# Reciprocals of softmax sums spread over partitions by DMA in a two-layer transformer kernel

## What is computed

```python
def _L0_attn_ref(x, norm_scale, wq, wk, wv, w_out, b_out):
    h = _rmsnorm(x, norm_scale)
    q = jnp.einsum('bsd,dhe->bshe', h, wq)
    k = jnp.einsum('bsd,dhe->bshe', h, wk)
    v = jnp.einsum('bsd,dhe->bshe', h, wv)
    q = (q * scale).astype(softmax_dtype)
    weights = jnp.einsum('bqhd,bkhd->bhqk', q, kf)
    weights = jax.nn.softmax(weights, axis=-1).astype(dtype)
    new_vals = jnp.einsum('bhqk,bkhd->bqhd', weights, v).astype(dtype)
    out = jnp.einsum('bqhe,hed->bqd', new_vals, w_out) + b_out
    return out
```

## Time and profile before

| | |
|---|---|
| median of 3 runs | 1432.15 us (1431.54 to 1432.47) |
| the profiled execution's own time | 1431.51 us |
| its span, first to last instruction | 1429.7 us |
| instructions | 33458 |
| period of the main loop | 84.85 us |
| TensorE's granted clock, mean | 0.988 of full speed |

### The profile page before, as it was taken

The page is one execution under the profiler, slowest core; times in us unless marked ns, Lnnn a source line. Parts: engine busy times, 40 slices in busy tenths (PEclk is TensorE's granted clock), DMA queues, the critical chain, the costliest instruction groups (busy, mean ns, idle before and its releaser), DMA issues.

```text
span 1429.7 us, 33458 instructions
## 1 busy us (share of the span) xinstructions
PE 1366.9 (96%) x11456; PEld 1202.2 (84%) x11456; DVE 925.6 (65%) x2535; ACT 904.3 (63%) x2492; POOL 502.5 (35%) x409
## 2 busy tenths in 40 slices
PE   6897999999999999999999999999999999999867
PEld 4685989888898988889898898988889898888767
DVE  4366576675766757566675757667576675756684
ACT  6675766757577575766657576675757657575423
POOL 3307062350705316071440706235070531607100
PEclk9999999999999999999999999999999999999988
DMA  7000000000000000000000000000000000000000
GB/s 262 5 1 5 1 2 8 0 7 0 0 7 0 7 0 0 7 0 7 0 7 0 0 7 0 7 0 7 0 0 7 0 7 0 0 5 1 5 1 8
DMA packets 13944, 13.77 MB, mean 10 GB/s; under 512 B 1609, under 2 KB 12754, under 8 KB 13650
## 3 DMA queue, kind: packets, MB, share of 16 engines
q1 hardware_dynamic: 13906, 13.27, 2.9%
HBM read 11.17 MB, written 2.10 MB: 9 GB/s over the span
## 4 chain that ended last, share of the span: by engine, by line
PE 64%; issue 11%; DVE 8%; ACT 4%; DVEq 4%; POOL 3%; POOLq 2%; SPq 1%; DMA 1%; ACTq 0%
PE bank_F L1208 14%; PE bank_S L1081 6%; DVEq L346 4%; PE bank_T L1067 4%; PE bank_T L1122 4%; PE bank_A L1135 4%; PE bank_T L1068 3%; PE bank_T L1069 3%; PE bank_F L1067 3%; ACT probs L573 3%; PE bank_F L1068 3%; PE bank_F L1069 3%; PE bank_A L1146 3%; PE bank_A L1067 3%; PE bank_A L1068 3%
## 5 line engine op out<-in xcount | busy, mean ns | idle before, releaser
L1208 PE MATMUL bank_F<-down,hid 128*128 128x128 f32 x2944 | 357.5, 277 | 5.4 <-DVE x L790 4.6
L1208 PEld LDWEIGHTS bank_F<-down,hid 128*128 128x128 f32 x2944 | 342.0, 192 | 14.7 <-DVE x L790 8.3
L573 ACT ACTIVATE probs<-bank_S,neg_max 128x256 f32<-128x256 f32 x512 | 236.2, 476 | 140.7 <-DVE neg_max L711 140.7
L711 DVE TENSOR_REDUCE neg_max<-bank_S 128x2 f32<-128x512 f32 x256 | 164.6, 684 | 96.1 <-PE bank_S L1081 96.0
L790 DVE SCALAR_TENSOR_TENSOR x<-bank_F,gates,x 128x128 f32<-128x128 f32 x496 | 149.8, 343 | 42.5 <-PE bank_F L1208 32.6
L491 POOL TENSOR_TENSOR hid<-hid,qkv 128x1024 f32<-128x1024 f32 x60 | 169.2, 2831 | 22.6 <-ACT hid L589 22.6
L461 POOL TENSOR_TENSOR mean_sq<-sum_sq,one_over_d 128x2 f32<-128x2 f32 x16 | 3.1, 197 | 442.8 <-ACT h_row L547 442.8
L552 ACT ACTIVATE probsT<-bank_T 128x512 f32<-128x512 f32 x256 | 139.6, 606 | 27.8 <-PE bank_T L1122 27.8
L479 POOL TENSOR_TENSOR hid<-qkv 128x1024 f32<-128x1024 f32 x45 | 121.1, 2690 | 69.3 <-ACT qkv L552 69.3
L1146 PE MATMUL bank_A<-probsT,values 128*64 128x256 f32 x1024 | 139.6, 394 | 1.1 <-ACT probsT L552 1.0
L1122 PE MATMUL bank_T<-ident,probs 128*128 128x128 f32 x1024 | 138.3, 278 | 0.2 <-ACT probs L573 0.2
(11 more groups left out here) (187 smaller groups left out, 3133.2 us busy)
## 6 DMA issues: line engine op xcount, KB each, us to landing
x_row<-in_x SPq DMA_DIRECT2D x16, 128.0 KB, 2.2
hid<-in_w SPq DMA_DIRECT2D x1, 2048.0 KB, 9.1
down<-in_w SPq DMA_DIRECT2D x1, 2048.0 KB, 14.3
out<-x SPq DMA_DIRECT2D x16, 128.0 KB, 1.8
hid<-in_rw SPq DMA_DIRECT2D x1, 1024.0 KB, 7.3
hid<-in_wv SPq DMA_DIRECT2D x1, 512.0 KB, 3.9
hid<-in_wq SPq DMA_DIRECT2D x1, 512.0 KB, 5.1
hid<-in_wk SPq DMA_DIRECT2D x1, 512.0 KB, 5.8
```

Source lines behind the costliest of these rows:

```text
L573: ins = sc.activation(probs[:, h // 2 % 2, h % 2, t, :], unit.bank(f"S{h}")[:, t * S:(t + 1) * S], ACT.Exp, bias=neg_max[:, h, t:t + 1], a ...
L711: ve.tensor_reduce(neg_max[:, h, :], v.bank(f"S{h}")[:, :].rearrange("p (t k) -> p t k", t=NT), AX.X, ALU.max, negate=True).then_inc(max_r ...
L1208: ins = te.matmul(bank[:, (j * NT + t) * P:(j * NT + t + 1) * P], hid[:, e, k, tokens(t)], down[:, e, k, :], start=k == 0, stop=k == m - 1)
```

## The change

The reciprocals no longer go through ScalarE and TensorE. SP stores `sum_inv` of a pair (128 partitions x 4 values) to a small DRAM buffer, `sums_apart`, so that the 256 tokens of each head lie one behind the other there. Once this store has landed, SP loads each head's 256 values to 64 partitions (a source step of 0), two loads per pair, into `inv_spread`. VectorE's `o_scale` then multiplies the bank of `O` directly with `inv_spread` and writes `oT`. Both buffers have two slots, by the parity of s. `o_out`, `repeat_inverse` and `spread` are gone with their semaphores, and VectorE's reciprocal waits until the store of two pairs ago has landed. SP's body is written out for all 18 iterations in place of the hardware loop. The two loads of 2 MB move from SP's `load_late` to ScalarE, behind the first pair's copies in iteration 0.

```diff
-        row_inv = sb("row_inv", P, 2, NT, 2, DH)
+        sums_apart = nc.dram_tensor("sums_apart", [2, 2, S], F32).ap()
+        inv_spread = sb("inv_spread", P, 2, S)
...
-                load(4, up1_loaded, w1_in)
-                load(4, down1[:], w2_in)
+
+            def spread_inverse(v, s):
+
+                sp.wait_ge(inverse_ready, v.at(0, HP, s + 1))
+                if v.it > 0 or s >= 2:
+                    sp.wait_ge(inverse_spread, v.at(0, 32 * HP, 32 * max(s - 1, 0)))
+                sp.dma_start(sums_apart[s % 2].rearrange("j (t p) -> p (j t)", t=NT), sum_inv[:, s % 2, :], allow_slow_non_contiguous=True).then_inc(inverse_stored, 16)
+                sp.wait_ge(inverse_stored, v.at(0, 16 * HP, 16 * (s + 1)))
+                if s >= 2:
+                    sp.wait_ge(*v.drain(f"O{s - 2}"))
+                elif v.it > 0:
+                    sp.wait_ge(*v.previous().drain(f"O{HP - 2 + s}"))
+                for j in range(2):
+                    src = sums_apart[s % 2, j]
+                    sp.dma_start(inv_spread[j * DH:(j + 1) * DH, s % 2, :], bass.AP(src.tensor, src.offset, [[0, DH], [1, S]])).then_inc(inverse_spread, 16)
...
+                if v.a:
+                    for s in range(HP):
+                        spread_inverse(v, s)
                 if v.c:
                     sp.wait_ge(ln_ready[3], v.at(2, 1, 1))
...
-            run(sp, body)
+            for it in range(ROWS + 2):
+                body(Iteration(it, 0, banks))
...
-            def o_out(v, s):
-
-                act.wait_ge(*v.fill(f"O{s}"))
-                sc.activation(oT(s), v.bank(f"O{s}")[:, 0:S], ACT.Copy).then_inc(o_copied, 1)
...
-            def repeat_inverse(v, s):
-
-                act.wait_ge(inverse_ready, v.at(0, HP, s + 1))
-                sc.activation(row_inv[:, s % 2], sum_inv[:, s % 2].rearrange("p (j t a) -> p t j a", j=2, a=1).broadcast_to([P, NT, 2, DH]),
-                              ACT.Copy).then_inc(repeated_ready, 1)
...
                     if v.a and s == HP - 2:
-                        o_out(v, s - 1)
-                        repeat_inverse(v, s)
                         transposed_probs(v, s)
...
+                    if v.it == 0 and s == 0:
+                        for dst, src in loads1:
+                            act.dma_start(dst, src).then_inc(loaded[4], 16)
...
+                if v.it > 0 or s >= 2:
+                    dve.wait_ge(inverse_stored, v.at(0, 16 * HP, 16 * max(s - 1, 0)))
                 settled(dve, ve.reciprocal(sum_inv[:, s % 2, :], row_sum[:, s % 2, :]).then_inc(inverse_ready, 1))
...
-                dve.wait_ge(o_copied, v.at(0, HP, s + 1))
-                ve.tensor_tensor(oT(s), oT(s), v.bank(f"O{s}")[:, S:2 * S], ALU.mult).then_inc(v.drain(f"O{s}")[0], 1)
+                dve.wait_ge(*v.fill(f"O{s}"))
+                dve.wait_ge(inverse_spread, v.at(0, 32 * HP, 32 * (s + 1)))
+                ve.tensor_tensor(oT(s), v.bank(f"O{s}")[:, 0:S], inv_spread[:, s % 2, :], ALU.mult).then_inc(v.drain(f"O{s}")[0], 1)
...
-            def spread(v, s):
-
-                bank = v.bank(f"O{s}")
-                pe.wait_ge(*v.drain(f"O{s}", before=1))
-                pe.wait_ge(repeated_ready, v.at(0, HP, s + 1))
-                for t in range(NT):
-                    te.transpose(bank[:, S + t * P:S + (t + 1) * P], row_inv[:, s % 2, t].rearrange("p j e -> p (j e)"), ident[:])
...
-                    if name[0] == "S" and bank == "S0" and v.nth.get(f"O{int(name[1:]) // 2 - 2}"):
-                        spread(v, int(name[1:]) // 2 - 2)
```

More of the change, by code:

```diff
@@ L314, in transformer_blocks @@
         inverse_ready = sem("inverse_ready")
-        repeated_ready = sem("repeated_ready")
-        o_copied = sem("o_copied")
+        inverse_stored = sem("inverse_stored")
+        inverse_spread = sem("inverse_spread")
         max_ready = sem("max_ready")
@@ L362, in weights_and_values @@
                     qkv1[:, t, :, 2, :].rearrange("p g (a d) -> p a d g", a=1).broadcast_to(full))
-        n_loads = [0] * 5
+        loads1 = (up1_loaded, w1_in), (down1[:], w2_in)
+        n_loads = [0, 0, 0, 0, 16 * len(loads1)]
         def wait_weights(eng, v, group):
@@ L654, in body @@
                         softmax_exp(v, 2 * s + 3)
-                    if v.a and s >= 1 and s != HP - 2:
-                        o_out(v, s - 1)
-                    if v.a and s != HP - 2:
-                        repeat_inverse(v, s)
                     if v.b and s == 1:
@@ L673, in body @@
                     head_exp(v, 1)
-                if v.a:
-                    o_out(v, HP - 1)
                 sc.activation(table_load[:], table_load[:], ACT.Gelu)
@@ L1138, in unit @@
                     s = int(name[1:])
-                    if s >= HP - 2:
-                        spread(v, s)
                     for j in range(2):
```

## The result

The changed kernel takes 2094.6 us (median of 4 runs, 2086.16 to 2100.63), against 1432.31 us before (1431.54 to 1433.03): 1.462 times as long, 95% interval 1.4567 to 1.4672. The forecast was 1394, with a range to 1418. It is 662 us slower, where 38 us faster was forecast.

What follows compares the result with a forecast made beforehand. TensorE was taken to bound the loops. Removed transposes 32 us, the output projection's wait 3 and the first row 3 made 38 us off 1431.5, forecast 1394 us as the runs' median, range 1379 to 1418.

Steps and rivals of the forecast that it cites:

- What the removed transposes cost: Main loop, TensorE: removing two `spread` transposes per head pair saves 1.98 us per row, 32 us over 16 rows.
- The alternative of 40 us: TensorE, same transposes: if the 0.09 us behind each `spread` went as well, removal would save 40 us.
- What bounds the kernel: Main loop: TensorE is busy 84.41 of 84.85 us per period, so work taken off it comes off the time.
- GpSimd: Near-full stretch up to the first norm: expected to follow; as rival floor (chance 0.12) loses 14 us, giving 1408.
- not on the path: Rival, chance 0.05: some order among engines sets the period, and freed time returns as waits, 1431 us.
- The price of the store: SP's store of 512 single values to DRAM: 2.6 us to landing, ends 1.8 and 8.4.
- The loads: SP's loads of reciprocals to 64 partitions: 2.2 us from issue to landing, taken from a row's load.
- Is L hidden?: Between reciprocal and scaling: 9.9 us of room for pair 0, 9.6 for pair 7, so 5.8 fits.
- L: Per pair, time from the start of the reciprocal to the loads' landing: 5.8 us, ends 5.0 to 11.6.
- the chain becomes the bound: Rival, chance 0.06: `o_scale` waits for pairs 0 and 7; slower from L = 10.9, 1454 us at L = 11.6.
- First row: First row: `spread` waits of 2.7 us go, moved weight loads lose 0 to 14; together gain 3, range -8 to +6.
- The sum: Whole kernel: 32 + 3 + 3 = 38 us off 1431.5 gives 1393.5, with the runs' median 1394.

Runs made afterwards that it cites:

- the probe: Kernel without the computation: SP issues and awaits small DMAs alone, three times each; the change's store took 9.41 to 10.30 us.
- the run with late weights: Changed kernel storing 16 B rows (wrong order), SP loading the experts' first matrix ahead of iteration 0's pairs, other late weights behind: 1395.03 us.
- The best kernel that divides rightly: Against the run with late weights: each half of the partitions loads all 512 values, single slot, `o_scale` reads every fourth column; 1411.98 us.

## Why the prediction was wrong, and where it was right

**What the removed transposes cost: right.** 1.98 us per row were worked out from the spacing of starts. Without the chain TensorE is busy for 1.96 us less per period, and the period is 2.03 shorter. The alternative of 40 us (the 0.09 of each unit going too) was wrong.

**What bounds the kernel, GpSimd, "not on the path": right.** Once the chain is out of the way, TensorE is busy for 82.45 of 82.82 us, and GpSimd follows.

**The price of the store: wrong, and this is the step that failed.** "I take 2.6, since nscale with its 128 pieces takes no longer than a row of 128 KB", with ends 1.8 and 8.4. It measured 9.4 to 10.3 alone and 9.86 in the kernel, above even the upper end. nscale's row is a load, out of DRAM and into 128 partitions. The new transfer writes pieces into DRAM, side by side. Reading 512 such pieces costs 2.13 us and writing them 9.4 to 10.3, so the row was taken from the wrong direction. I had set aside the rule that I quoted from the Trainium skill ("DMA: Bandwidth & Descriptors", Anatomy of one DMA, a surprisingly long wait for writes to HBM) because whole rows land quickly. For whole rows that was right: four of 512 B are written in 1.16 us and 128 of 16 B in 1.4 to 2.0. For the change's store it was not. Its packets are over within 1.63 us of the issue, and for the other 8.20 us SP waits with the DMA engines at 0.00, which agrees with that rule. The rule gives no price by which the two kinds of store could be told apart. The same page's rule on transfers under 512 B (Specifications: read, modify and write) points the right way, but by itself it does not tell 16 B rows at 1.4 to 2.0 us from 4 B pieces at 9 to 10. What the runs show is the spacing of the pieces. There was also a warning against this change that I had not weighed: the Trainium skill ("VectorE: DVE Perf Modes", The three transpose paths) calls a plain DMA that transposes by its access pattern a trap when the innermost step in the destination is large. The change's store has such a step, 512 B between the values of one partition, and its 9.4 to 10.3 us agree. But it is not this step that makes it slow. The probe's fast stores have even larger ones (8 KB and 64 KB, 1.8 to 2.8 us), and 128 values with no inner step at all take 7.4 to 9.6; the slow step is the 4 B between neighbouring partitions.

**The loads: off by over a half.** 2.2 was taken, 3.6 measured in the changed kernel (median), 2.8 behind a second issue in the probe. With the fast store the chain still fits: the run with late weights has no wait for it to speak of.

**"Is L hidden?": wrong in kind.** It priced only the lateness of pairs 0 and 7, as if every pair started afresh. SP serves the pairs one behind the other. Its time per pair was compared with 5.9 in one clause ("SP itself is held for about 3.8 us per pair"), yet the rival had no price for the case that it exceeds it. That case has no slack: each microsecond over 5.9 comes back seven times per row. The rival "the chain becomes the bound" gave 1454 us at its upper end of L = 11.6. By its own rule L = 15.6 would have given (5.7 + 6.0 - 2.3) x 16 = 150 us, some 1580. By the throughput of SP, seven times (11.03 - 5.9) is 36 us per row, 575 in all, and 2.0 of it is paid back by the transposes. The measured 2094.6 lies beyond that by what comes behind the last store of a row, 7.0 us in the row shown. The experiments with extra stores show the multiplication at work without the slow store: two of them per pair, at 2.2 us each on the mean, cost 259 us.

**The clock: not foreseen.** The prediction held TensorE's work constant. Behind the waits the same eight matmuls took 1.98 us instead of 1.08, at a granted clock of 0.50. By the estimate above this is some 1.8 us of the 42.8 per row.

**First row: wrong in sign, inside its range.** A gain of 3 was taken, from -8 to +6. With whole rows stored, the first finished row comes at 231.37 against 231.93 before, 0.6 us earlier, though three iterations have lost their transposes by then, 2.0 us each: a net loss of 5. The moved loads make it, 9.3 us (231.37 to 222.07), of which 6.7 appear only together with the small transfers (231.37 to 224.65), in the way that the prediction named: the second lands late (20.6 us instead of 14.3), amid the new small transfers, which wait beside it.

**The sum.** With the store at 16 B per row and the weights moved, the measured 1395.0 stands beside the forecast 1394. So the sum was right but for two terms, both DMAs: the store's price with what it does to SP, and the moved loads. That holds for a kernel whose reciprocals lie in the wrong order. The best kernel that divides rightly takes 1411.98, since putting them in order costs something too, for which the prediction had no term besides the store.

## What to carry to other kernels

Before a small transfer is put on a path, time it alone in its own direction and with its own layout in DRAM: here 64 to 512 single values 4 B apart in DRAM cost 7 to 10 us to write, and 16 of them 1.9 to 2.5, while 128 rows of 16 B or more cost 1.4 to 2. Then ask two questions of the chain and not one: does its latency fit the slack, and does the time that its serving engine spends per item fit the items' spacing? In this kernel an excess of service time was paid once per item, by the table above; that an excess of latency is paid only once per deadline is the prediction's picture, and no run tests it alone. Where an order in memory has to change, a stepped read or a transposition on an engine with idle time can be cheaper than letting the DMA do it, but even 0.2 us on each use can show in the time when that engine stands between two units of the bound one.

## What the hardware showed that I had not expected

- Writing single values of 4 B to DRAM costs by how densely they lie: 128 values at a step of 4, 8, 16 and 32 B took 7.4 to 9.6, 3.3 to 4.6, 1.9 to 2.1 and 1.4 to 1.9 us. At a step of 4 B, 16 values took 1.9 to 2.5 and four 1.1. Reading 512 at a step of 4 B took 2.13.
- Of the 9.86 us of such a store in the kernel, its packets are over within the first 1.63; in the 8.20 behind them the DMA engines' share is 0.00.
- A load of other data issued 0.5 us behind such a store on the same queue was complete only 11 us later, though the DMA engines were nearly done with its packets in 3 us.
- A store of 128 rows of 16 B took 1.4 us in a quiet loop and 11.19 us beside two loads of 2 MB.
- The same multiplication on VectorE, 128x256, took 0.42 us with its second operand contiguous and 0.61 us with a step of four values.
